# The mixture-of-experts stage in 64-row tiles: two experts a product, shared experts one chunk ahead, halves added by a product

## The reference

```python
for s in range(shared_w.shape[0]):                       # 2 shared experts
    shared = shared + _gelu(_c1(feats, shared_w[s], shared_b[s])) / shared_w.shape[0]
...
gate_w = jnp.zeros((B, NUM_EXPERTS), x.dtype).at[jnp.arange(B)[:, None], idx].add(wts)   # TOP_K = 4 of 16
out = shared
for e in range(NUM_EXPERTS):
    out = out + _gelu(_c1(feats, expert_w[e], expert_b[e])) * gate_w[:, e][:, None, None, None]
return out + residual
```

## Time and profile before

| | us |
|---|---|
| median of 3 runs | 7533.4 |
| lowest, highest | 7525.0, 7562.55 |
| the profiled execution: device time | 7550.36 |
| the profiled execution: span of the trace | 7548.5 |
| stage `experts`, first DMA issue to the first DMA issue of the next stage | 2644.5 to 3024.7 |
| of it: masks and sums of the weights on DVE | 2653.9 to 2684.7 |
| of it: main loop, first product to last addition | 2684.8 to 3020.9 |

### The profile page before, as it was taken

One profiled execution on the slowest core, in us unless ns is written; L12 is line 12 of the kernel. 1 busy time (PEld: TensorE's weight loads), 2 busy tenths in 40 slices (PEclk: granted clock), 3 DMA queues, 4 the chain that ended last, 5 costly groups with the idle time before them and its releaser, 6 DMA issues. The chain is left out here.

```text
span 7548.5 us, 120463 instructions
## 1 busy us (share of the span) xinstructions
PE 6575.4 (87%) x36560; PEld 3443.7 (46%) x36560; DVE 5590.7 (74%) x5630; ACT 3977.8 (53%) x6794; POOL 3832.4 (51%) x2716
## 2 busy tenths in 40 slices
PE   8968699999967379687999999999989999999970
PEld 7852233333345134574222222222257777777750
DVE  4653677777712278103999999999979999999974
ACT  4424466666612457103666666666655555555532
POOL 0100122222200300002888888888879999999960
PEclk9989799999978689757999999999989999999985
DMA  2243234334355523533222222222200000000016
GB/s 70 72 169 124 68 99 100 100 99 101 96 127 151 229 81 100 130 86 56 37 37 36 37 37 37 39 39 38 29 16 10 10 10 10 10 10 10 8 40 190
DMA packets 638233, 518.91 MB, mean 69 GB/s; under 512 B 249981, under 2 KB 569251, under 8 KB 629563
## 3 DMA queue, kind: packets, MB, share of 16 engines
q1 hardware_dynamic: 637947, 515.62, 27.9%
HBM read 304.91 MB, written 171.32 MB: 63 GB/s over the span
## 5 line engine op out<-in xcount | busy, mean ns | idle before, releaser
L2582 DVE TENSOR_TENSOR_SCAN spa_hs<-spa_p_d,spa_hs,spa_bx 128x483 f32<-128x483 f32 x1168 | 1370.3, 1223 | 21.1 <-ACT spa_p_d L2495 21.1
L2302 POOL TENSOR_TENSOR spa_hc<-spa_hs,spa_cr 128x966 f32<-128x966 f32 x592 | 1219.0, 2069 | 240.7 <-DVE spa_hs L2582 239.3
L2725 POOL TENSOR_TENSOR spe_hc<-spe_hs,spe_bcu 128x1024 f32<-128x1024 f32 x520 | 1219.7, 2362 | 64.5 <-DVE spe_hs L2937 63.5
L2937 DVE TENSOR_TENSOR_SCAN spe_hs<-spe_p_d,spe_bx 128x1024 f32<-128x1024 f32 x520 | 1161.4, 2275 | 35.0 <-ACT spe_p_d L2885 31.7
L2812 PEld LDWEIGHTS spe_p_y<-spe_idt,spe_hc 128*128 128x128 f32 x8320 | 965.1, 192 | 143.8 <-issue 143.8
L1065 DVE TENSOR_REDUCE attention_nm<-attention_p_s 128x2 f32<-128x640 f32 x1024 | 789.1, 812 | 260.2 <-PE attention_p_s L922 259.1
L2812 PE MATMUL spe_p_y<-spe_idt,spe_hc 128*128 128x128 f32 x8320 | 978.2, 276 | 0.0
L1023 ACT ACTIVATE attention_pr<-attention_p_t 128x512 f32<-128x512 f32 x1280 | 710.7, 599 | 420.3 <-PE attention_p_t L945 289.1
L2495 ACT ACTIVATE spa_p_d<-spa_p_d,spa_av 128x483 f32<-128x483 f32 x1184 | 703.9, 633 | 428.3 <-PE spa_p_d L2366 426.2
L2885 ACT ACTIVATE spe_p_d<-spe_p_d 128x896 f32<-128x896 f32 x520 | 445.5, 900 | 759.1 <-PE spe_p_d L2795 758.8
L2366 PE MATMUL spa_p_d<-spa_du,spa_hot 32*128 32x483 f32 x2368 | 657.0, 630 | 56.5 <-DVE spa_hs L2582 48.4
(11 more groups left out here) (425 smaller groups left out, 10630.8 us busy)
## 6 DMA issues: line engine op xcount, KB each, us to landing
attention_qs<-scratch_qp SPq DMA_DIRECT2D x768, 64.0 KB, 2.8
spa_uc<-spa_du SPq DMA_DIRECT2D x148, 241.5 KB
attention_rc<-scratch_den SPq DMA_DIRECT2D x128, 256.0 KB
scratch_qp<-patch_parts SPq DMA_DIRECT2D x64, 384.0 KB, 2.3
spa_xt<-scratch_x SPq DMA_DIRECT2D x148, 121.5 KB, 2.7
front_xs<-in_x_dram SPq DMA_DIRECT2D x64, 256.0 KB, 3.0
scratch_xf<-front_out SPq DMA_DIRECT2D x128, 128.0 KB, 2.5
patch_x<-scratch_xf SPq DMA_DIRECT2D x8, 2048.0 KB, 19.8
```

Of the source, the lines that this page charges most:

```text
L2302: nc.gpsimd.tensor_tensor(hc[:, k % 8:k % 8 + 2, :], hs[:, k:k + 2, :], cr2[:, s % 2, :].unsqueeze(1).broadcast_to([128, 2, NA]), ALU.mult ...
L2582: nc.vector.tensor_tensor_scan(hs[:, k, v], p_d[k % 4][:, v], bx[:, k, v], 0.0 if start else hs[:, k, NA - 1:NA], ALU.mult, ALU.add).then_ ...
L2725: nc.gpsimd.tensor_tensor(hc[:, k, :, d, :].rearrange("p s d t -> p d s t"), hs[:, k % 2, d, :, :], rows, ALU.mult)\
L2937: nc.vector.tensor_tensor_scan(hs[:, k % 2, d].rearrange("p d s t -> p (d s t)"), p_d[h][:, :], bx[:, k % 2, d].rearrange("p d s t -> p (d ...
```

## The change

Only `experts` and the layouts of its weights change; `after` and `stream` move up in the file. What it now does:

- **Products.** For each chunk and each image half p (partitions 64p to 64p+63) there are three products of 64 rows x 128 columns x 512 pixels: one makes both shared experts (`wsh`), one makes chosen experts 0 and 1, one makes 2 and 3 (`wx`). So the 128 outputs are two experts of one image. The six products of a chunk use full matrices, with no zero half. The two of a pair stand on different 64-row halves of TensorE's array, into different PSUM tiles `p_x[k][p]`.
- **Fold.** The two experts of one image stand on different partition halves of `acc`. A product with `fold` (two 64 x 64 unit matrices, one above the other; 128 rows x 64 columns) adds the halves into `p_o`, two a chunk (p = 0, 1), on the two column halves. DVE then adds the residual (`finish`).
- **Shared experts.** ACT writes them to `gs` in SBUF, POOL multiplies them by 1/2 into `us`, and DVE starts the sum from `us`. Their products run one chunk ahead.
- **DVE** has four multiply-adds and one addition a chunk, before six multiply-adds. **ACT** has six GELUs as before.
- **Order.** `stream` sets it: step i has the products 0/1 of chunk i-1, the shared ones of chunk i, the products 2/3 of chunk i-1, the fold of chunk i-2; on DVE first additions of i-1, `finish` of i-2, last additions of i-1. Chunks go alternately to the two pairs, four a turn; `feats` has four buffers, and stores follow five steps behind the loads.
- **Selection.** The sums go over all 128 partitions at once: 8 sums, before 16; 4 of the 8 masks are made by POOL. Loads of constants are 13, before 14; the gates `gx` come as single 4-byte elements.

```diff
@@ -1802,100 +1830,125 @@
...
-        p_x = [st.ps(f"p_x{k}", [128, 512]) for k in range(NX)]
-        loaded, zeroed, step, w_ready = st.sem("loaded"), st.sem("zeroed"), st.sem("step"), st.sem("w_ready")
-        f_in, x_done, x_ready = st.sem2("f_in"), st.sem("x_done"), st.sem("x_ready")
-        summed = [st.sem(f"summed{k}") for k in range(NX)]
-        stored = st.sem2("stored")
-        N = NF // 2
+        p_x = [[st.ps(f"p_x{k}{p}", [128, 512]) for p in range(2)] for k in range(NP)]
+        p_o = [st.ps(f"p_o{s}", [128, 512]) for s in range(2)]
...
+            for p in range(2):
                 for a in range(2):
-                    b = 2 * q + a
+                    b = 2 * a + p
+                    sp.dma_start(hot[64 * p:64 * p + 64, a].rearrange("p k e -> p (k e)"),
...
+            def load(c, s, r):
+                after(sp, x_done, 4 * (c - 3))
+                sp.dma_start(fs[:, s, :], feats[:, s % 2, columns(s, r)]).then_inc(f_in[s], 16)
+            def store(c, s, r):
+                sp.wait_ge(out_ready, c + 1)
+                sp.dma_start(ov[:, s % 2, columns(s, r)], os[:, s % 2, :]).then_inc(stored[s % 2], 16)
+            stream(sp, NCH, UX, 2 * UX, 5, (0, load), (5, store))
...
+        @block.tensor
+        def _(pe):
+            def spread_shared(c, s, r):
+                pe.wait_ge(f_in[s], 16 * r + 16)
+                for p in range(2):
+                    after(pe, shared_active, 2 * c + (p - 1))
+                    rows = slice(64 * p, 64 * p + 64)
+                    nc.tensor.matmul(p_x[1][p][:, :], wsh[rows, :], fs[rows, s, :], start=True, stop=True).then_inc(shared_done, 1)
+            def spread(k, free):
+                def run(c, s, r):
+                    for p in range(2):
+                        after(pe, free, 2 * c + (p - 1))
+                        rows = slice(64 * p, 64 * p + 64)
+                        nc.tensor.matmul(p_x[k][p][:, :], wx[rows, s % 2, k // 2, :], fs[rows, s, :], start=True, stop=True).then_inc(x_done, 1)
+                return run
+            def add_halves(c, s, r):
+                after(pe, out_ready, c - 1)
+                for p in range(2):
+                    pe.wait_ge(last_added, 2 * c + (p + 1))
+                    mm = nc.tensor.matmul(p_o[s % 2][64 * p:64 * p + 64, :], fold[:, :], acc[:, s % 2, p, :], start=True, stop=True)
+                mm.then_inc(folded, 1)
+            pe.wait_ge(loaded, 16 * 13)
+            pe.wait_ge(w_ready, 2 * TOP + 2)
+            stream(pe, NCH, UX, UX, 2, (1, spread(0, first_added)), (0, spread_shared), (1, spread(2, last_added)), (2, add_halves))
...
+            def activate_shared(c, s, r):
+                for p in range(2):
+                    act.wait_ge(shared_done, 2 * c + (p + 1))
+                    after(act, shared_scaled, 2 * c + (p - 3))
+                    nc.scalar.activation(gs[:, s % 2, p, :], p_x[1][p][:, :], ACT.Gelu, bias=bsh[:, 0:1]).then_inc(shared_active, 1)
+            def activate(k, active):
+                def run(c, s, r):
+                    for p in range(2):
+                        b = 2 * (s % 2) + p
+                        act.wait_ge(x_done, 4 * c + (k + p + 1))
+                        nc.scalar.activation(p_x[k][p][:, :], p_x[k][p][:, :], ACT.Gelu, bias=bx[:, b, k // 2:k // 2 + 1]).then_inc(active, 1)
+                return run
+            act.wait_ge(w_ready, 2 * TOP + 2)
+            stream(act, NCH, UX, UX, 1, (1, activate(0, first_active)), (0, activate_shared), (1, activate(2, last_active)))
...
-                        for k in range(NX):
-                            pe.wait_ge(summed[k], n)
-                            mm = nc.tensor.matmul(p_x[k][:, :], wx[:, a, k, :], fs[:, s, :], start=True, stop=True)
...
-                    link(nc.vector.tensor_tensor(pk[:, :, :], wes[:, :, :], hot[:, a, k, :].unsqueeze(1).broadcast_to([128, C, NE]), ALU.mult))
-                    for q in range(2):
-                        r = slice(64 * q, 64 * q + 64)
-                        last = nc.vector.tensor_reduce(wx[r, a, NSH + k, 64 * q:64 * q + 64], pk[r], AX.X, ALU.add)
-                        link(last)
...
-                            part = os[:, s, :] if k else hr[:, a, bass.ds((2 * j + s) * 512, 512)]
-                            nc.vector.scalar_tensor_tensor(os[:, s, :], p_x[k][:, :], gx[:, a, k:k + 1], part,
-                                                           ALU.mult, ALU.add).then_inc(summed[k], 1)
+            def choose(a, k, t):
+                nc.vector.tensor_reduce(wx[:, a, k // 2, C * (k % 2):C * (k % 2) + C], pk[:, t], AX.X, ALU.add).then_inc(w_ready, 1)
+            dve.wait_ge(loaded, 16 * 13)
+            nc.vector.tensor_tensor(fold[:, :], idt[:, 0:C], idt[:, C:2 * C], ALU.add).then_inc(w_ready, 1)
+            link(nc.vector.tensor_tensor(pb[:, :, :], hot2[:, :, :], bes[:, :].unsqueeze(1).broadcast_to([128, B * TOP // 2, NE]), ALU.mult))
+            nc.vector.tensor_reduce(bx[:, :, :].rearrange("p b k -> p (b k)"), pb[:, :, :], AX.X, ALU.add).then_inc(w_ready, 1)
+            for i in range(TOP):
+                for t in range(2):
+                    a, k = (2 * i + t) // TOP, (2 * i + t) % TOP
+                    if t == 0:
+                        if i:
+                            dve.wait_ge(w_ready, 2 * i + 1)
+                        link(nc.vector.tensor_tensor(pk[:, 0], wes[:, :, :], hot[:, a, k, :].unsqueeze(1).broadcast_to([128, C, NE]), ALU.mult))
+                    else:
+                        dve.wait_ge(halved, i + 1)
+                    choose(a, k, t)
+            def add_first(c, s, r):
+                t, b = s % 2, lambda p: 2 * (s % 2) + p
+                for p in range(2):
+                    dve.wait_ge(first_active, 2 * c + (p + 1))
+                    dve.wait_ge(shared_scaled, 2 * c + (p + 1))
+                    after(dve, folded, c - 1)
+                    nc.vector.scalar_tensor_tensor(acc[:, t, p, :], p_x[0][p][:, :], gx[:, b(p), 0:1], us[:, t, p, :], ALU.mult,
+                                                   ALU.add).then_inc(first_added, 1)
+            def add_last(c, s, r):
+                t, b = s % 2, lambda p: 2 * (s % 2) + p
+                for p in range(2):
+                    dve.wait_ge(last_active, 2 * c + (p + 1))
+                    dve.wait_ge(first_added, 2 * c + (p + 1))
+                    nc.vector.scalar_tensor_tensor(acc[:, t, p, :], p_x[2][p][:, :], gx[:, b(p), 1:2], acc[:, t, p, :], ALU.mult,
+                                                   ALU.add).then_inc(last_added, 1)
+            def finish(c, s, r):
+                dve.wait_ge(folded, c + 1)
+                after(dve, stored[s % 2], 16 * (r * 2 + s // 2))
+                nc.vector.tensor_tensor(os[:, s % 2, :], p_o[s % 2][:, :], hr[:, s % 2, columns(s, r)], ALU.add).then_inc(out_ready, 1)
+            stream(dve, NCH, UX, UX, 2, (1, add_first), (2, finish), (1, add_last))
+        @block.gpsimd
+        def _(pool):
+            def scale(c, s, r):
+                for p in range(2):
+                    pool.wait_ge(shared_active, 2 * c + (p + 1))
+                    after(pool, first_added, 2 * c + (p - 3))
+                    nc.gpsimd.tensor_tensor(us[:, s % 2, p, :], gs[:, s % 2, p, :], share[:, :], ALU.mult).then_inc(shared_scaled, 1)
+            nc.gpsimd.memset(share[:, :], 1.0 / NSH).then_inc(filled, 1)
+            pool.wait_ge(loaded, 16 * 13)
+            pool.wait_ge(filled, 1)
+            for i in range(TOP):
+                a, k = (2 * i + 1) // TOP, (2 * i + 1) % TOP
+                if i:
+                    pool.wait_ge(w_ready, 2 * i + 2)
+                nc.gpsimd.tensor_tensor(pk[:, 1], wes[:, :, :], hot[:, a, k, :].unsqueeze(1).broadcast_to([128, C, NE]), ALU.mult)\
+                    .then_inc(halved, 1)
+            stream(pool, NCH, UX, UX, 0, (0, scale))
```

157 lines of the change are left out of this document (55 added, 102 removed).

## The result

| | us |
|---|---|
| before, median of the runs beside it | 7534.8 (7525.0 to 7562.6) |
| after, median | 7493.9 (7471.7 to 7507.0) |
| ratio | 0.9936, 95% interval 0.9913 to 0.9958 |
| forecast | 7476, range 7448 to 7515 |

The change makes the program 0.64% faster, 41 us by the medians (32 to 66 by the interval). The profiled execution of after took 7507.0 us, that of before 7550.4.

A forecast was written before the change was run, and what follows sets the result against it. The prediction took TensorE to bound the loop before, and a circle of waits of 4.45 us a chunk after. Loop -43 and selection -15 from the median 7533.4 gave, with the clearing, 7476 us, range 7448 to 7515.

The forecast's parts named there:

- a circle: Main loop: waits through `finish`, last additions, second product and fold set 4.45 us a chunk, above busy times of 3.7 to 4.0.
- The pairs run side by side: TensorE: two 64-row products take the time of one, 0.866 us; the rival of no pairing, 7588 us and more, had chance 0.05.
- come just in time: Main loop, ACT: the GELUs of 2/3 must follow the product by 1.3 us and have little slack.
- the longer circle: Rival, main loop: GELUs, first additions or blocking products lengthen the circle to 4.8 to 5.1 us a chunk, 7498 to 7517; chance 0.21.
- the shorter: Rival, main loop: early weight loads and free tiling changes leave busy times, 3.75 to 4.2 us a chunk, 7431 to 7460; chance 0.10.
- The loop as a whole: Main loop: 64 x 4.45 = 284.8 us plus filling, together 292.8 against 336.1, so -43 us.
- The loads: Stage start: `gx` and `hot2` in 512 small pieces each can cost or save 2 us, taken as 0.
- The selection: Selection before the loop: 15.8 us of DVE against 30.8, POOL's masks hidden with nothing to spare, -15 us.
- a side case with -10: Selection: if masks of POOL and DVE keep each other waiting, 5 us are lost and the gain is -10.
- the forecast case: Main case for the whole program: 4.25 to 4.7 us a chunk, 7463 to 7492 us; chance 0.58.
- PE busy 100%: Profile sign in the main loop, listed among those that would show the forecast wrong.
- The slow clock as a rival: Rival: TensorE, fed 78%, is granted clock 0.5, 7662 us; decides from 0.45 of the loop at low clock; chance 0.06.

The follow-up runs named there:

- Finish last: Changed kernel with DVE's `finish` moved behind the last additions of the step: 3.84 us a chunk against 4.39, loop 252.9 us against 288.6.
- the runs on one half: Changed kernel with the second products of all pairs, or only of pair 2/3, on the first's 64 rows: 12.38 and 4.64 us a chunk, against 4.39.
- Gates as whole rows: Changed kernel with the gates loaded as contiguous rows of 16 numbers and picked by two DVE copies: loads 9.2 us against 19.3, loop 287.4.
- all pairs on one half: Changed kernel with both products of every pair on partitions 0 to 63: 12.38 us a chunk against 4.39, loop 798.8 us, granted clock 0.50.

## Why the prediction was right where it was right, and where it failed

**What bounds the kernel, and that it would be a circle: right.** The predicted steps against one turn in the trace:

| part of the circle | forecast | measured |
|---|---|---|
| `finish` to the last additions | 0.68 | 0.61 |
| two last additions | 1.50 - 0.16 for both overlaps | 1.40 |
| DVE to TensorE | 0.05 | 0.05 |
| second product, change to column tiles | 1.07 | 1.05 |
| fold | 1.08 | 1.08 |
| TensorE to DVE, register steps | 0.23 | 0.16 and 0.26 by turns |
| sum | 4.45 | 4.35 and 4.46 by turns |

Each term came from a row of the kernel before, of this stage or another, but for 0.20 of the last one, which was put between 0.1 and 0.3, and none is off by more than 0.07. "Finish last" shows that the circle was the bound and not only as long as the bound: cut there, the chunk falls to what the prediction gave as TensorE's own occupation, 3.7 to 3.9, and in every other step the circle through the GELUs adds some 0.12 us.

**The pairs run side by side: right.** The 32-row rows of the spatial stage carried over to 64-row tiles of 128 columns: the runs on one half show what it would be without. The gap at a change of tiling, read as up to 0.2 us, is 0.10 into the fold's tiling, 0.15 out of it and 0.10 once more behind the pair that follows, where TensorE waits for nobody; the two changes cost about 0.36 of the 3.78 us of such a step. The section "Key Properties" of the Trainium skill's page "TensorEngine Tiling (Array Packing)" has it that such a change drains the engine, and the gaps agree.

**The GELUs of 2/3 "come just in time": too dark.** They start at 2824.69 and the first is done by 2825.37, while the additions that need them start behind the `finish` of 2825.92. That was the ground for giving the longer circle twice the chance of the shorter. It costs nothing in the number, but the slack of over 1 us was to be had from the same sum.

**The loop as a whole, -43.3: the forecast term was 4.2 us too small.** 64 x 0.06 = 3.8 of it is the chunk; the start cost 288.6 - 64 x 4.39 = 7.6 us, forecast 8.0.

**The loads, "which can cost or save 2 us, taken as 0": the step that failed, +9.8.** The prediction named the 512 small pieces and gave them 2 us either way, from no row. "Gates as whole rows" shows that the gates' two DMAs cost 10.0 us. The nearest rows of before would not have warned: the gates came as rows of four numbers in 2.3 us, and the 512 single elements of `spa_jump` in 2.1 to 2.4. What no row had is this form of a DMA, every other number of a row read one by one and over again for each of 64 partitions. I put it at the price of its neighbours, with a range of 2 us where nothing bounded it above. Why the two together are slow, where neither is alone, stays open.

**The selection, -15: mis-sized, -10.6.** The prediction said that the mask of GpSimd would be "hidden, with nothing to spare", and gave the contention as a side case with -10. Measured are 20.3 us: about 5.1 are lost to contention, 2.15 of them at the product for the biases, and without it DVE's own work is 15.2, forecast 15.8. The rule of the Trainium skill (page "SBUF — State Buffer", section "Who interferes with whom"), that a DVE instruction with two SBUF inputs contends with a GpSimd one that reads SBUF, gave the right outcome, and the traces above agree with it: together 3.25 instead of 2.38, and beside one-input sums 2.35. It should have been the forecast. The trace of before had no row for it either way, and the price of being wrong was all on one side.

**The sum.** +9.8 and +4.4 against -4.2 and some tenths: -47.9 instead of -57.4 in the stage. The time came out 18 us above the forecast; 9.5 of it are these terms, and the rest is within what the medians tell (interval of the ratio: 17 us up or down). It lies in the range, but 2 us above the 7463 to 7492 of the forecast case, although the chunk lies inside that case's 4.25 to 4.7. The range reached there for a longer circle, which didn't come; that it also held the error of the loads is luck.

**A sign and the ground of a rival were badly chosen.** "PE busy 100%" was to mean that the pairs don't run side by side; PE was at 99.9%, and they do. Records last until the result is out, two tiles cover each other's gaps, and so busy time hides slack in a kernel with tiles. The slow clock as a rival was priced by how busy TensorE is; "all pairs on one half" has it busy all the time and at 0.50. That rival's "0.45 of the loop" is also too high: at its 2.9 us a chunk the gain of 58 us is gone after 58 / 186 = 0.31 of the loop.

## What to carry to other kernels

- When the wait table shows each engine waiting for the next in every turn, walk the circle step by step and look for the instruction that stands in a queue ahead of work that doesn't need it. Here moving one addition behind two others gave 35 us, nearly three quarters of what the whole rewrite of the loop had given. Then check by how much another circle is shorter: moving the fold instead gave 4 us (64 x 0.07).
- An operation that the trace doesn't show has no safe price from its neighbour: 512 single elements landed in 2.2 us in one form and in 6.6 and more in another. For a form of DMA without a row and for GpSimd beside two-input DVE operations take the bad end, or arrange the work so that they don't occur: whole rows and a pick on chip, masks beside sums.
- Saved changes of tiling are worth it only if the longer block doesn't starve the engines behind TensorE.
